# Macaron block on one core: the taps' transforms of single blocks, joined in neighbouring pairs by VectorE with an alternating sign

## What is computed

```
x = x + 0.5 * ffn(layernorm(x))          # 256 -> 1024 -> 1024 -> 1024 -> 256, ternary weights
x = x + gelu(fftconv(layernorm(x), K)) @ W.T + b
x = x + 0.5 * ffn(layernorm(x))

K[d, l] = 2 * Re(sum_n C[d, n] * exp(dtA[d, n] * l))      # the "taps", 256 channels x 1024
y = irfft(rfft(x_t, 2048) * rfft(K, 2048))[:, :, :1024]   # a causal convolution over l
```

## Time and profile before

| | before |
|---|---|
| median of 3 runs | 1329.17 us (1328.3 to 1329.56) |
| the profiled execution, its own time | 1328.43 us |
| its span in the profile | 1326.6 us |
| PE busy | 1315.0 us (99%) |
| DVE busy | 867.3 us (65%) |
| ACT busy | 746.3 us (56%) |
| POOL busy | 402.9 us (30%) |
| mean granted TensorE clock | 0.998 of full |

### The profile page before, as it was taken

How to read it: one execution, slowest core, us unless ns; L and a number is a source line. 1 busy time by engine, 2 the same in 40 slices (tenths; PEclk the granted TensorE clock), 3 DMA queues, 4 the chain that set the end, 5 groups by cost and what they waited for, 6 DMA issues and landing times.

```text
span 1326.6 us, 18338 instructions
## 1 busy us (share of the span) xinstructions
PE 1315.0 (99%) x7278; PEld 670.0 (51%) x7278; DVE 867.3 (65%) x1703; ACT 746.3 (56%) x1201; POOL 402.9 (30%) x394
## 2 busy tenths in 40 slices
PE   8999999999999999999999999999999999999998
PEld 3454454644545445455454554545545455454544
DVE  5277767423455876978779787787877874454633
ACT  4665457645356566673765736657467464545432
POOL 6721377600012422623226233261432600001000
PEclk9999999999999999999999999999999999999999
DMA  8310000000010000000100000000010002231400
GB/s 309 135 40 9 8 1 17 1 9 9 0 56 9 8 10 1 16 1 1 16 1 17 9 9 17 17 8 17 8 17 17 8 17 72 56 104 34 157 1 18
DMA packets 44701, 41.88 MB, mean 32 GB/s; under 512 B 32704, under 2 KB 41408, under 8 KB 41920
## 3 DMA queue, kind: packets, MB, share of 16 engines
q1 hardware_dynamic: 44320, 40.54, 10.2%
q10 hardware_dynamic: 288, 0.10, 0.0%
HBM read 28.57 MB, written 4.19 MB: 25 GB/s over the span
## 4 chain that ended last, share of the span: by engine, by line
PE 96%; ACT 1%; DVE 1%; DMA 0%; issue 0%; DVEq 0%
PE psf L1345 65%; PE psf L1333 17%; PE psf L1357 8%; PE pss L1408 2%; PE pss L1418 2%; PE pss L1398 2%; PE pss L1373 1%; PE pss L1388 1%; ACT g L1154 1%; DMA scr<-sc 0%; DVE arena L804 0%; ACT psf L1115 0%; ACT hab L1108 0%; DVE arena L801 0%; DVE xr L657 0%
## 5 line engine op out<-in xcount | busy, mean ns | idle before, releaser
L1345 PE MATMUL psf<-hab,wall 128*128 128x512 f16 x4096 | 890.9, 379 | 2.4 <-DVE ht L640 0.9
L1345 PEld LDWEIGHTS psf<-hab,wall 128*128 128x128 f16 x4096 | 399.3, 98 | 483.4 <-issue 5.2
L1115 ACT ACTIVATE psf<-psf,scf 128x512 f32<-128x512 f32 x256 | 168.7, 659 | 430.0 <-PE psf L1345 429.9
L628 DVE SCALAR_TENSOR_TENSOR hab<-psf,hab 128x512 f16<-128x512 f32 x256 | 175.3, 687 | 317.4 <-ACT hab L1108 317.1
L1333 PE MATMUL psf<-h,wall 128*128 128x512 f16 x1024 | 232.9, 381 | 0.7 <-ACT h L1119 0.7
L1333 PEld LDWEIGHTS psf<-h,wall 128*128 128x128 f16 x1024 | 99.8, 98 | 117.1 <-issue 1.9
L1108 ACT ACTIVATE hab<-psf 128x512 f16<-128x512 f32 x256 | 152.8, 597 | 8.1
L972 POOL TENSOR_SCALAR rs<-mv 128x4 f32<-128x4 f32 x16 | 3.1, 194 | 468.4 <-DVE mv L671 468.4
L640 DVE SCALAR_TENSOR_TENSOR ht<-psf,scf,sil 128x512 f32<-128x512 f32 x128 | 95.0, 749 | 72.4 <-PE psf L1333 69.9
L1098 ACT ACTIVATE sil<-psf,scf 128x512 f32<-128x512 f32 x128 | 87.1, 685 | 90.6 <-PE psf L1333 88.5
L628 DVE SCALAR_TENSOR_TENSOR hab<-ht,hab 128x512 f16<-128x512 f32 x128 | 118.1, 931 | 3.0
(11 more groups left out here) (131 smaller groups left out, 904.3 us busy)
## 6 DMA issues: line engine op xcount, KB each, us to landing
arena<-wh SPq DMA_DIRECT2D x8, 1024.0 KB, 5.6
g<-wh SPq DMA_DIRECT2D x6, 1024.0 KB, 8.6
out<-xr SPq DMA_DIRECT2D x15, 256.0 KB, 2.2
xr<-x SPq DMA_DIRECT2D x7, 512.0 KB, 5.1
arena<-w SPq DMA_DIRECT2D x3, 1024.0 KB, 5.5
g<-w SPq DMA_DIRECT2D x2, 1024.0 KB, 7.0
xr<-wh SPq DMA_DIRECT2D x2, 1024.0 KB, 9.6
g<-w SPq DMA_DIRECT2D x2, 512.0 KB, 6.7
```

What stands on the lines that cost most here:

```text
L628: e.scalar_tensor_tensor(out=hab[:, buffer(p), m, 1, :], in0=source(p), scalar=2.0 ** E2 if l else 1.0, in1=hab[:, buffer(p), m, 0, :], op ...
L1115: e.activation(bank, bank, ACT.Gelu, scale=scf[:, 2 + l, m:m + 1]).then_inc(s_gelu, 1)
L1345: ins = e.matmul(bank[:, :], WH[:, l, m // 2, k, ms], hab[:, buffer(p), k, part, :], start=(k == 0 and part == 0), stop=(k == KH - 1 and p ...
```

## The change

The linearity of the transform is used in another place. PE transforms each block of taps by itself, always as the first half of a window, with 3 matmuls of 512 columns a part. Moving a block by 128 places in a window of 256 multiplies frequency `f` by (-1)^f, so the window's transform is block `j-1`'s plus (-1)^f times block `j`'s. ACT copies both parts of every call to SBUF, into two arrays of 9 x 256 columns (`blocks`) whose first 256 are zero; DVE adds the pair with the sign as a scalar of each partition (a new column of the constants), and then makes the same three combinations as before, from SBUF alone. The slots of the calls are changed too.

```diff
+C_SIGN = 152
...
+    c[:, C_SIGN] = alt
...
-SPECTRUM_AT = T(3, 13), T(3, 15), T(3, 20), T(3, 23)
-IMAGINARY_AT = T(3, 14), T(3, 16), T(3, 22), T(3, 25)
-SPECTRUM_OUT_AT = T(3, 15), T(3, 20), T(4, 2), T(4, 3)
+SPECTRUM_AT = T(3, 13), T(3, 15), T(3, 22), T(3, 24)
+SPECTRUM_COPY_AT = T(3, 14), T(3, 20), T(3, 23), T(3, 25)
+SPECTRUM_OUT_AT = T(3, 25), T(3, 25), T(4, 2), T(4, 3)
...
+        blocks = [arena[:, 3072 + 2304 * i:5376 + 2304 * i] for i in range(2)]
         gds = [small[:, 0:512], small[:, 512:1024]]
+        paired = gds
...
             def taps_low():
                 w.wait_ge(s_half, 4)
+                for part in blocks:
+                    ch.done(e.memset(part[:, 0:D], 0.0))
...
-                bc, gd = pss[q % 2], gds[q % 2]
-                w.wait_ge(s_spec, 2 * q + 2)
-                w.wait_ge(s_gd, q + 1)
-                ch.done(e.tensor_scalar(go[0], bc[:, :], msk, None, ALU.mult))
-                ch.done(e.scalar_tensor_tensor(
-                    out=go[1], in0=bc[:, :], scalar=nms, in1=gd, op0=ALU.mult, op1=ALU.add))
+                bc, gd = paired
+                w.wait_ge(s_gd, 2 * q + 2)
+                ch.after()
+                for part, to in zip(blocks, paired):
+                    ch.done(e.scalar_tensor_tensor(
+                        out=to, in0=part[:, D * (2 * q + 1):D * (2 * q + 3)], scalar=sign,
+                        in1=part[:, D * 2 * q:D * (2 * q + 2)], op0=ALU.mult, op1=ALU.add))
+                ch.after()
+                ch.done(e.tensor_scalar(go[0], bc, msk, None, ALU.mult))
+                ch.done(e.scalar_tensor_tensor(out=go[1], in0=bc, scalar=nms, in1=gd, op0=ALU.mult, op1=ALU.add))
                 mark["gd", q] = now["slot"], ch.done(e.scalar_tensor_tensor(
-                    out=go[2], in0=gd, scalar=msk, in1=bc[:, :], op0=ALU.mult, op1=ALU.add))
-                return 2250
+                    out=go[2], in0=gd, scalar=msk, in1=bc, op0=ALU.mult, op1=ALU.add))
+                return 3600
...
             def spectrum(q):
-                w.wait_ge(s_spec, 2 * q + 2)
-                if q > 1:
-                    w.wait_ge(s_dve, mark["gd", q - 2][1])
-                e.activation(gds[q % 2], pss[2][:, :], ACT.Copy).then_inc(s_gd, 1)
+                for n, bank in enumerate((pss[q % 2], pss[2])):
+                    w.wait_ge(s_spec, 2 * q + n + 1)
+                    e.activation(blocks[n][:, D * (2 * q + 1):D * (2 * q + 3)], bank[:, :], ACT.Copy).then_inc(s_gd, 1)
...
                 for n in range(2):
-                    bank = side(2, s_gd, q + 1) if n else side(q % 2, s_dve, mark["gd", q][1])
-                    w0 = P * 2 * n
-                    for lo, hi in ((0, 2),) if q else ((0, 1), (1, 2)):
-                        js = slice(2 * q + lo, 2 * q + hi)
-                        steps = [(w0 + P, js)] + [(w0, slice(js.start - 1, js.stop - 1))] * (js.start > 0)
-                        steps = [(at, j, hw, hk) for at, j in steps for hw, hk in MIX]
-                        for o, (at, j, hw, hk) in enumerate(steps):
-                            ins = e.matmul(bank[:, D * lo:D * hi], win16[:, hw, at:at + P],
-                                           k16[:, hk, D * j.start:D * j.stop], start=(o == 0),
-                                           stop=(o == len(steps) - 1))
+                    bank = side(2 if n else q % 2, s_gd, 2 * q + n + 1)
+                    for o, (hw, hk) in enumerate(MIX):
+                        ins = e.matmul(bank[:, :], win16[:, hw, 2 * P * n:2 * P * n + P],
+                                       k16[:, hk, 2 * D * q:2 * D * (q + 1)], start=(o == 0), stop=(o == 2))
                     ins.then_inc(s_spec, 1)
```

More of the change, by code:

```diff
@@ L747, in spectrum @@
             def spectrum(q):
-                msk, nms = cs[:, C_MASK:C_MASK + 1], cs[:, C_NMASK:C_NMASK + 1]
+                msk, nms, sign = (cs[:, c:c + 1] for c in (C_MASK, C_NMASK, C_SIGN))
                 go = [g3[:, i, 2 * q:2 * q + 2, :].rearrange("p j d -> p (j d)") for i in range(3)]
-                bc, gd = pss[q % 2], gds[q % 2]
-                w.wait_ge(s_spec, 2 * q + 2)
-                w.wait_ge(s_gd, q + 1)
-                ch.done(e.tensor_scalar(go[0], bc[:, :], msk, None, ALU.mult))
-                ch.done(e.scalar_tensor_tensor(
-                    out=go[1], in0=bc[:, :], scalar=nms, in1=gd, op0=ALU.mult, op1=ALU.add))
+                bc, gd = paired
[8 more added lines that the diff above has]
+                ch.done(e.scalar_tensor_tensor(out=go[1], in0=bc, scalar=nms, in1=gd, op0=ALU.mult, op1=ALU.add))
                 mark["gd", q] = now["slot"], ch.done(e.scalar_tensor_tensor(
-                    out=go[2], in0=gd, scalar=msk, in1=bc[:, :], op0=ALU.mult, op1=ALU.add))
-                return 2250
+                    out=go[2], in0=gd, scalar=msk, in1=bc, op0=ALU.mult, op1=ALU.add))
+                return 3600
             def conv_sums(b, part):
@@ L872, in fixed @@
                     time += taps_low()
-                if t in SPECTRUM_OUT_AT:
-                    time += spectrum(SPECTRUM_OUT_AT.index(t))
+                for q in range(4):
+                    if t == SPECTRUM_OUT_AT[q]:
+                        time += spectrum(q)
                 u = i - FIRST
@@ L1240, in slot @@
                     taps_high()
-                if t in IMAGINARY_AT:
-                    spectrum(IMAGINARY_AT.index(t))
+                if t in SPECTRUM_COPY_AT:
+                    spectrum(SPECTRUM_COPY_AT.index(t))
                 u = i - FIRST
```

## The result

| | before | changed |
|---|---|---|
| median of 6 runs each | 1328.74 us (1327.44 to 1329.56) | 1323.88 us (1322.62 to 1324.47) |
| the profiled execution, its own time | 1328.43 us | 1324.47 us |
| its span in the profile | 1326.6 us | 1322.7 us |
| PE matmuls, busy | 7278, 1315.0 us | 7248, 1310.3 us |
| DVE busy | 867.3 us | 873.3 us |

The ratio of the times is 0.9964 (95% interval 0.9952 to 0.9976): 0.36% less. The changed kernel is faster, and 1324.6 had been predicted.

The account below looks back on a forecast made before the run. PE's matmuls were taken as the bound, with DVE's and ACT's added work hidden. The median 1329.17 less PE's 4.56 us gave 1324.6 us; the range was 1323.4 to 1326.8, full gain alone 1323.6 to 1325.6.

Parts of the forecast that it names:

- PE's part: Tap transforms ahead of pass 4: 24 matmuls of 512 columns, 5.18 us instead of 9.74, so 4.56 us less.
- A call of DVE: DVE's work per transform call: five instructions from SBUF, 3.5 us, with bounds of 3.0 and 8.2 us.
- First low half of pass 4: DVE's first two calls end at 359.8, before this low half is ready at 361.5: hidden, 1.7 us to spare.
- Slot 8: Pass 4, tightest place: DVE done with slot 5's low half at 376.8, PE asks at 378.2; 1.4 us lead.
- ACT's copies: The second copy ends at 324.8, PE's second call needs `pss[2]` at 326.5: 1.7 us of lead.
- The memsets: Two memsets of 256 columns, 0.27 us each, ahead of the taps' low part; 1.1 us of lead left.
- Each 0.1 us a call above costs PE 0.2 us.: Pass 4's slot 8: DVE calls longer than 4.2 us make PE wait 0.2 us per 0.1 us of excess.
- rival 2: DVE and POOL on SBUF at once stretch DVE's instructions; at 8.2 us a call 9.9 us slower, 1339.1; chance 0.03.
- Rival 1: DVE late at slot 8 of pass 4: at 4.7 us a call PE waits 1.0 us, 1325.6; chance 0.07.
- Rival 3: ACT's copies late, PE waits for `pss[2]`; each us over 1.7 costs one, 1 us lost gives 1325.6; chance 0.03.
- Rival 5: Matmuls in a mixed stream cost less than 215.8 ns; at 152 ns the gain is 3.2 us, 1326.0; chance 0.01.
- Rival 4: Gain given back in passes 5 to 12, where convolutions share DVE and POOL; 3 us lost gives 1327.6; chance 0.06.

## Why the prediction was right

- **PE's part.** 24 matmuls were put at 5.18 us and stand in the chain as 4 x 1.29 = 5.16. The stretch shrank by 4.55 us where 4.56 was worked out. The slots alone gave nothing, doubling the matmuls took nearly the whole gain away (5.18 us in the chain), and a third of them gave 3.46 us more: this is the cause, and it is shown. The spacing of 131 ns that the Trainium skill gives ("TensorE: Matmul & The Clock Gate", "Back-to-back issue gap") for streams of weight load and matmul is contradicted by 215.8 ns a matmul in both directions; the same section's formula for the isolated gap gives 216 ns, and that is what the rows have.
- **A call of DVE.** 3.5 us were predicted and 3.17 measured, nearer to the lower bound of 3.0. What failed was the scalar operation: it was put at 0.66 as the others, though the row of 382 ns for 428 columns had said that from SBUF alone it is shorter. It takes 0.49, the next one 0.40 behind it; from PSUM it took 0.746. The Trainium skill, "VectorE: DVE Perf Modes", section "The perf-mode tier table (the rule you actually need)", gives a 2x mode for such an operation on fp32 in SBUF and none from PSUM; the rows agree that it is shorter, though not by half.
- **The leads.** First low half of pass 4: 1.7 us predicted, 2.14 measured. Slot 8: 1.4 predicted, 2.1 measured; the difference is twice the 0.33 us that a call was shorter. ACT's copies: 1.7 predicted, 1.8 measured. The memsets: the low half of the taps ends at 317.53, PE begins at 318.65, 1.1 us as predicted. The runs with two and four extra instructions met PE at the very place named, with 1.17 and 4.33 us.
- **"Each 0.1 us a call above costs PE 0.2 us."** Right but for some 0.2 us at short waits, wrong for long ones. This step left out that the clock can fall on a long wait: 4.33 us of wait cost 6.2, and 1.7 of that is the clock. For the forecast this changed nothing, as there was no wait. It makes rival 2 worse than it was priced.
- **Rival 1** (DVE late at slot 8) did not happen; the run with two instructions more a call (3.17 + 2 x 0.79 = 4.75 us a call, near the 4.7 that the rival names) shows it near its price: 1.0 us had been named, and PE lost 1.3.
- **Rival 2** (DVE and POOL at once on SBUF) did not happen, for the reason given, since POOL has nothing to do there. The mechanism is real: forced, it made the kernel 0.50% slower than before. Its upper bound of 8.2 us a call was too low; 11.4 were measured. It came from a misreading. The row of 1641 ns, which the earlier trace rows calls the slowest of this shape, is a group of one; the 128 low halves with two SBUF inputs have the same shape, and their mean over the whole span is higher than the 685 ns of the eight in the earlier trace rows. From the page, and from the timelines of DVE and POOL, of the kernel before:

```profile
L628 DVE SCALAR_TENSOR_TENSOR hab<-ht,hab 128x512 f16<-128x512 f32 x128 | 118.1, 931 | 3.0
```

```profile
510.72 2.55 DVE L628 SCALAR_TENSOR_TENSOR hab<-ht,hab 128x512 f16<-128x512 f32 x1
```

```profile
510.32 2.40 POOL L1033 TENSOR_TENSOR arena<-arena,g 128x896 f32<-128x896 f32 x1
```

So single instructions reached 2.55 us beside POOL before any change. Five of them would have been a bound of 12.8 us a call, above the 11.4 measured. A mean hides such instructions. The rival was therefore priced too low as well. PE was stopped at slot 5, three slots ahead of the place that was named.
- **Rival 3** (ACT's copies late): no wait before the second call. **Rival 5** (the cheaper matmul, priced at 152 ns): refuted, above.
- **Rival 4** (the gain given back in passes 5 to 12): refuted by the distance between the two profiles, 3.98 us at 512 and 3.95 at 1255 us. Between pass 5 and 6 the chain even won some 0.35 us. PE stands still there for 0.48 us before, waiting for a gate of DVE, and for 0.14 us after. Of what stands ahead of it, ACT's first activation (514.01 and 510.39) is 3.62 us earlier in the changed kernel, as PE's up blocks are, and DVE's gate behind it (515.15 and 511.18) is 3.97 us earlier, so the 0.35 us arise between these two. Every kernel made from the changed one takes 81.62 us from pass 5's first hidden matmul to pass 6's, before and the one with the slots alone 81.97. What decides this was not found and no run was made for it; it stays open.
- **The time.** 1324.6 was the median shown, 1329.17, less 4.56. The measured 1323.88 is 0.7 lower. 0.43 of it is that before's own median of six runs is 1328.74, and the other 0.3 is about the size of the piece between pass 5 and 6, for which the forecast had no term; with scatter of 1 to 2 us between runs this last split is not shown by the medians. That one could tell only 0.2% from no change was too cautious: the interval came out 0.12% to either side.

## What to carry to other kernels

When one engine is the chain in a stretch, the gain of work taken off it is its count times its price from the rows, and the real question is the lead of the others: work it out at the place where the first engine asks, and compare it with the work added between there and the last idle time. Work given to DVE in SBUF is only cheap while POOL is quiet, so look at both in the same window. A forecast of a wait of several us should add what the lower clock takes from the matmuls behind it (1.7 and 1.4 us here). And before a slowest case is taken from a group's mean, look at the longest single instruction of the groups of the same shape.

## What the runs showed of the hardware

- A wait of 4.33 us of PE was followed by some 3 us of the 1.2 GHz level that began after PE had restarted, and cost 1.7 us on top. In a wait of 7.91 us the level was reached while PE still waited, and cost 1.4 us on top. Behind waits of 0.96 and 1.17 us the clock stayed at its full level.
- DVE instructions of 128x512 with two SBUF inputs went from 0.75 to 2.38 us beside POOL instructions that read SBUF, the scalar operation from 0.49 to 2.00, and POOL's own from 1.89 to 2.22. Both engines then started most of their instructions 2.3 us apart. With one input in PSUM one of DVE's stayed at 0.69.
- The start of the same kernel differs from run to run: in its two profiles, pass 4 began at 351.54 and at 350.75 us, with the clock at 0.50 for a time before 15 us in the first and at 1.00 throughout in the second.
